# TensorE's counting of edge sources: a loop of span bodies in place of 1,568 written-out tiles

## What is computed

```python
# layer 0
out_deg = maximum(segment_sum(ones, src), 1.0)
t1  = feat @ W1
msg = t1[src] + (feat[src] * feat[dst]) @ W2
msg = msg / (sqrt(out_deg[src]) * sqrt(out_deg[dst]))
embed = leaky_relu(where(in_cnt > 0, t1 + segment_sum(msg, dst), 0) + b)
x = layernorm(x + embed / norm(embed))
# layer 1
xt  = x @ W.T + b
out = segment_sum(xt[src], dst) / (deg + 1)
x = layernorm(x + out)
```

## Time and profile before

| what | before |
|---|---|
| median of three runs | 3994.8 us |
| the profiled execution | 3996.79 us |
| its span | 3995.1 us |
| PE busy | 2991.8 us, 75% |
| DVE busy | 1864.8 us, 47% |
| ACT busy | 664.3 us, 17% |
| POOL busy | 2982.0 us, 75% |
| DMA, mean over the span | 146 GB/s, 582.43 MB |

### The profile page before, as it was taken

How to read it: one execution, slowest core, us unless ns; L and a number is a source line. 1 busy time by engine, 2 the same in 40 slices (tenths; PEclk the granted TensorE clock), 3 DMA queues, 4 the chain that set the end, 5 groups by cost and what they waited for, 6 DMA issues and landing times.

```text
span 3995.1 us, 42771 instructions
## 1 busy us (share of the span) xinstructions
PE 2991.8 (75%) x10186; PEld 1828.7 (46%) x10186; DVE 1864.8 (47%) x3536; ACT 664.3 (17%) x2054; POOL 2982.0 (75%) x3146
## 2 busy tenths in 40 slices
PE   4551777777777777777777877888888888878887
PEld 4441555555555555555433333344334343334443
DVE  9994555555555555555423333333333323232323
ACT  7992111111111111111100000000000000000000
POOL 7776777777777777777667777777777777777776
PEclk5555888988888888888867777666766666776667
DMA  8878455555555555555334443434443434343433
GB/s 256 272 233 309 150 156 155 155 156 155 156 155 155 156 158 156 158 155 156 116 94 118 117 118 116 119 115 120 115 120 115 120 115 120 115 121 114 120 115 107
DMA packets 294217, 582.43 MB, mean 146 GB/s; under 512 B 60723, under 2 KB 176100, under 8 KB 294180
## 3 DMA queue, kind: packets, MB, share of 16 engines
q0 software_dynamic: 150048, 409.93, 35.4%
q1 hardware_dynamic: 131364, 159.19, 11.9%
q10 hardware_dynamic: 12768, 12.85, 0.9%
HBM read 506.27 MB, written 75.45 MB: 146 GB/s over the span
## 4 chain that ended last, share of the span: by engine, by line
POOL 65%; issue 23%; POOLq 1%; PE 1%; DVE 0%; DVEq 0%; DMA 0%; ACT 0%; SPq 0%; ACTq 0%
POOL ring L478 65%; PE banks L1095 0%; POOLq L511 0%; DVEq L688 0%; POOLq L475 0%; PE banks L1121 0%; POOLq L476 0%; PE banks L1084 0%; DMA ring<-scaled_x,idx 0%; DMA ring<-x,idx 0%; POOL ring L488 0%; DMA x<-out_t 0%; DVE stats L917 0%; DVE out_t L929 0%; DVE big L850 0%
## 5 line engine op out<-in xcount | busy, mean ns | idle before, releaser
L1121 PE MATMUL banks<-ring,hot_space 128*128 128x257 f32 x6252 | 2470.7, 521 | 806.8 <-DMA ring<-x,idx 330.9
L1121 PEld LDWEIGHTS banks<-ring,hot_space 128*128 128x128 f32 x6252 | 1309.8, 242 | 1896.2 <-DMA ring<-x,idx 1058.0
L478 POOL DMA_INDIRECT ring<-x,idx x1563 | 1486.9, 951 | 505.3 <-issue 475.9
L478 POOL DMA_INDIRECT ring<-scaled_x,idx x1281 | 1221.2, 953 | 402.7 <-issue 402.7
L850 DVE SCALAR_TENSOR_TENSOR big<-banks,here_mask,big 128x257 f32 x784 | 343.9, 480 | 1604.5 <-PE banks L1121 1604.3
L806 DVE TENSOR_TENSOR hot_space<-banks,dst_rel 128x1024 f32<-128x1024 f32 x395 | 483.5, 1225 | 212.6 <-issue 210.8
L592 ACT COPY idx<-src_col 128x8 int32 (+1 forms) x392 | 77.3, 197 | 2145.7 <-PE banks L1121 2145.7
L488 POOL DMA_INDIRECT ring<-in_x,src_col x276 | 264.1, 957 | 84.1 <-issue 84.1
L554 ACT ACTIVATE dst_rel<-columns,halves 128x128 bf16<-128x128 f32 (+1 forms) x896 | 253.5, 374 | 23.8 <-PE banks L1042 19.6
L1035 PE MATMUL banks<-hot_space 128*128 128x98 bf16 x1120 | 104.2, 283 | 139.2 <-DVE hot_space L695 139.2
L1095 PE MATMUL banks<-w_s,a_t 128*128 128x256 f32 x784 | 179.3, 383 | 0.0
(11 more groups left out here) (115 smaller groups left out, 1193.2 us busy)
## 6 DMA issues: line engine op xcount, KB each, us to landing
kept_rows<-ring SPq DMA_DIRECT2D x94, 384.0 KB, 3.4
ring<-kept_rows SPq DMA_DIRECT2D x47, 768.0 KB, 5.5
ring<-x,idx POOLq DMA_INDIRECT x1563, 2.8
ring<-scaled_x,idx POOLq DMA_INDIRECT x1281, 2.8
dst_col<-in_src SPq DMA_DIRECT2D x47, 384.0 KB, 5.8
scaled_x<-big ACTq DMA_DIRECT2D x14, 896.0 KB, 17.5
x<-out_t SPq DMA_DIRECT2D x98, 128.0 KB, 2.4
x_t<-x SPq DMA_DIRECT2D x98, 128.0 KB, 2.3
```

The costliest lines, as they stand in the source:

```text
L478: g.indirect_dma_start(ring[:, u, 0:D], None, table[layer], bass.IndirectOffsetOnAxis(ap=idx[:, u:u + 1], axis=0)).then_inc(rows_in[u], 16)
L1121: last = nc.tensor.matmul(group_sum(k % SUMS), dst_hot[:, k % HOTS, u - k * GT, :], ring[:, u, 0:DW], start=u == tiles[0], stop=u == tiles ...
```

## The change

The order of PE's counting is rewritten as a span of two hot batches and three step batches: hot batch 2n, step batches 3n and 3n+1, hot batch 2n+1, step batch 3n+2. Span 0 is written out, spans 1 to 34 are a loop on PE, and the step batches that are left, 105 to 111, are written out behind it. What DVE, ACT, POOL and SP do, and in which order, is unchanged; `hot_made` and `steps_made` are now waited for against values that PE computes from the loop's counter.

```diff
-            for n in range(SRC_BATCHES):
-                hist_batch(n, n % 2, n == 0, False)
-                for k in range(n * STEP_BATCHES // SRC_BATCHES, (n + 1) * STEP_BATCHES // SRC_BATCHES):
-                    step_batch(k, k % 3, k == 0, k == STEP_BATCHES - 1)
+
+            def span(n, first):
+                for half in range(2):
+                    hist_batch(2 * n + half, half, first and half == 0, False)
+                    for third in ((0, 1), (2,))[half]:
+                        step_batch(3 * n + third, third, first and third == 0, False)
+
+            span(0, True)
+            with pe.Fori(1, SRC_BATCHES // 2) as n:
+                span(n, False)
+            for k in range(SRC_BATCHES // 2 * 3, STEP_BATCHES):
+                step_batch(k, k % 3, False, k == STEP_BATCHES - 1)
             pe.wait_ge(step_diffs_made, 1)
             nc.tensor.matmul(hist, between[:, :], step_rows[1], start=False, stop=True).then_inc(counts_whole, 1)
```

## The result

| | before | changed |
|---|---|---|
| median of 20 runs | 3995.11 us | 4000.93 us |
| the profiled execution | 3996.79 us | 4001.47 us |
| its span | 3995.1 us | 3999.7 us |
| step sums read by DVE | 294.86 us | 307.89 us |
| POOL's first gather of the layers | 374.21 us | 380.40 us |

The ratio is 1.0014, with a 95% interval of 1.0008 to 1.002: 5.8 us more by the medians; the interval leaves out 1, and the difference is within the 0.2% that the prediction counted as the same. The forecast was 5.4 us more, 4000.2 us, and its range of 3997 to 4006.5 us holds the result. The layers took 1.6 us less in this one profile; over the nine profiles of this study that stretch lay between 3617.4 and 3621.2 us, so single spans can't be compared more finely than that, and where a start moved is read from the timeline of the preparation.

A forecast was written before the change was run, and what follows sets the result against it. The prediction took POOL to bound the layers and DVE the count. The loop adds nothing; step sums come 12.4 us later, of which 5.4 us reach the layers: 3994.8 + 5.4 = 4000.2 us, range 3997 to 4006.5 us.

The forecast's parts named there:

- What bounds the kernel: Whole kernel: POOL sets the pace from its first layer gather; the change moves only that start, passed on one for one.
- The loop costs nothing: PE's count: a trip costs 0.8 us (0.4 to 1.3), covered by 3.9 us of spare time a trip.
- Rival B: PE's count loop: the branch back stalls PE on code fetches, 4017 us at 5 us a trip; chance 0.06.
- The order of the steps: Count's end: ACT makes seven late step batches one after another, so DVE reads the step sums 12.4 us later.
- Rival C: Count's end: the seven late step batches are hidden and nothing moves, 3994.8 us; chance 0.10.
- What reaches the layers: Table's store to POOL's first layer gather: of 12.4 us, between 4.8 and 6.2 us arrive, taken as 5.4 us.
- two accounts: Table's lateness: DMA engines freed beforehand, 5.8 us; or store falls 2.5 MB behind, made up alone, 6.5 to 7.2 us.
- The first account: Table's store: 2.6 MB out of the way beforehand, worth 6.6 us at 395 GB/s; table ends 5.8 us later.
- Rival A: Table's store: it does not catch up, staying near 205 GB/s when alone; 4006.2 us, chance 0.18.
- The slack of 1.0 us: Before the layers: table landed at 370.90, POOL released at 371.89, so the table may be 1.0 us later for nothing.

The follow-up runs named there:

- no_tail: The changed kernel's loop with one step batch behind it in place of seven, six left out of the count; 3994.65 us against 3996.0, ratio 0.9999.
- load_3: The changed kernel with three register loads on PE's sequencer added to each loop trip; 4003.09 us against 3996.29 for the kernel before, ratio 1.0019.
- load_8: The changed kernel with eight register loads on PE's sequencer added to each loop trip; 4018.2 us against 3996.29 for the kernel before, ratio 1.0054.
- order_only: The changed kernel's order of hot and step batches, all spans written out without the loop; 4000.41 us against 3996.0, ratio 1.0012.
- tail_14: The kernel before, no loop, with 14 step batches left behind the last hot batch; 4009.8 us against 3996.0, ratio 1.0038.
- steps_116: The kernel before, written out, with 116 step and 69 hot batches in place of 112 and 70; 3994.98 us against 3996.29, ratio 0.9995.

## Why the prediction was right

**What bounds the kernel: right.** Only the start of the layers moved, and the whole change in time is that start to within the scatter of the layers, 3617.4 to 3621.2 us.

**The loop costs nothing: right.** no_tail has the loop and not the time, load_3 has a dearer trip and not the time, and load_8 puts the point where it begins to cost at some 3.8 us a trip. What a trip does cost on PE's sequencer is in the changed kernel's rows for the loop's line (ns: least, median, most):

```profile
L1063 PEldq FUSED_REGOPS  x34: 50/50/50, 28.8 to 286.2; - x34
L1063 PEldq ALU_OP  x34: 32/32/32, 36.5 to 293.6; - x34
L1063 PEldq COMPARE_BRANCH  x34: 76/208/240, 36.6 to 293.7; - x34
```

0.05, 0.03 and 0.21 us, and with four more register instructions of some 0.03 us 0.4 us in all, where I took 0.8 from bounds of 0.4 and 1.3. It can't be seen in PE's waits: the second half of the loop's first trip, and the head of the next,

```profile
36.29 1.49 PE L1035 MATMUL banks<-hot_space 128*128 128x98 bf16 x16 [1.75 <-DVE hot_space L695]
37.58 0.53 PE L1042 MATMUL banks<-dst_rel 128*128 128x98 bf16 x4
40.19 1.49 PE L1035 MATMUL banks<-hot_space 128*128 128x98 bf16 x16 [2.08 <-DVE hot_space L695]
```

and PE waits for DVE at both hot batches, 1.75 us ahead of the one inside the trip and 2.08 ahead of the one behind the branch, as in the earlier trace rows. Rival B fell with this. The instruction packets of q8 over the span, before and after, went from 20 to 8, so the loop of 34 trips did not load its code again with every trip:

```profile
q8 instruction: 20, 0.33, 0.0%
...
q8 instruction: 8, 0.13, 0.0%
```

The rule of the Trainium skill (Runtime: NRT & Kernel Launch, section "Instruction fetch mechanics") speaks of a branch to code outside the two loaded blocks; this trace agrees that a short body is not such a case, and no run here had one that is.

**The order of the steps costs 12.4 us at the count's end: right.** Seven batches in 15.75 us (15.9 by the sum), the step sums at 307.17 in order_only (307.3). In the changed kernel's own profile it is 13.0 us, of which 0.7 were there before the count began. Rival C, that the late steps are hidden, fell with the first profile, and order_only with tail_14 shows the rule behind them: one ACT batch for each step batch that is left over, from the moment at which its third comes free.

**What reaches the layers, 5.4 us: right, with two prices off that offset each other.** In order_only, which has the forecast's delay (12.3 us), the table lands 7.0 us later and the first gather 5.5. The prediction's 5.4 is 6.4 us for the table, 0.6 too little, less 1.0 us of slack, where 1.45 is to be taken off, as below. That 5.4 came so near has some luck in it; in the changed kernel it was 6.2.

Of the two accounts, 5.8 and 6.5 to 7.2 us at the table, the second is borne out. It let the store fall 2.5 MB behind and make this up alone; the store was 2.44 MB behind at 360 us, and at the 341 GB/s of load_8 that takes 7.2 us, where the changed kernel took 7.64. Its price of a lone store, 350 to 390 GB/s from single microseconds, was too high. The first account has the engines at the full 395 GB/s to the end and is too low. The kept rows did not get out of the way sooner either: their last store landed at 373.74 us, 1.9 us later than before. For that reason one sign was missed: between 371 and 376 us q10 was to move over 300 GB/s and moved 1.42 MB, 284 GB/s, with 0.39 MB of q1 beside it. Rival A needed a lone store below 280 GB/s, and there is none.

**The slack of 1.0 us: half a microsecond too small.** Before, the last chunk landed at 370.87 us and the last kept rows at 371.81, 0.94 us behind, as the prediction read. But POOL then had waits of the table's chunks still to pass, one after another, and came to the last one, that of the last chunk, only at 372.35:

```profile
371.89 0.04 POOLq L501
...
372.35 0.04 POOLq L501
```

So the table could have landed some 1.5 us later for nothing. In the changed kernel these waits were passed while the table was on its way, the last chunk landed at 378.52 us and POOL went on at 378.54. For a gain the slack does not hold: the kept rows do not end at a time of their own, as was expected for steps_116, since they moved by 1.5 us there.

## What to carry to other kernels

When a written-out stream is folded into a loop, look first at what the round numbers of the loop's body do to the pace of each producer, and only then at the branch: here 1.5 step batches for a hot batch in place of 1.6 left seven for a producer that has only three buffers, and that was the whole cost. Spare time of an engine that waits for another covers a good deal of sequencer work, and it can be read from its busy time against the other's period. A delay ahead of a transfer that shares full DMA engines arrives only in part: the transfer loses what it would have moved beside the others (2.44 MB in 13.0 us here, 187 GB/s) and makes it up later at the rate that it has alone, 341 GB/s.

## What the runs showed of the hardware

A store of `scaled_x` alone on the DMA engines ran at 341 GB/s over 18 us (load_8), while the engines moved some 395 GB/s when three queues were active together; their share was 1.04 and 1.05, so they were full in both. A register load on PE's sequencer took 0.30 us in a row of loads and 0.48 us standing alone. A loop's compare-and-branch on PE took 0.21 us at the median. With eight register loads in each trip, where PE stood idle for some 4.6 us, its mean granted clock in the count rose from 0.50 to between 0.57 and 0.61.
